# A three-layer graph network by one level of Strassen: halves of 1354 columns and a reordered schedule

## The reference

```python
h = maximum(layernorm(x), 0)
h = relu(adj @ (h @ W1) + b1)
h = relu(adj @ (h @ W2) + b2)
out = x + adj @ (h @ W3) + b3
```

## Time and profile before

| | us |
|---|---|
| median of 3 runs (lowest, highest) | 1641.04 (1639.48, 1642.48) |
| the profiled execution | 1642.07 |
| its span, first to last instruction | 1639.0 |
| TensorE busy | 1595.6 (97%) |
| VectorE busy | 868.2 (53%) |
| ScalarE busy | 605.7 (37%) |
| GpSimd busy | 472.0 (29%) |
| mean granted TensorE clock | 0.992 |
| HBM traffic | 191 GB/s over the span |

### The profile page before, as it was taken

How to read it: one execution, slowest core, us unless ns; L and a number is a source line. 1 busy time by engine, 2 the same in 40 slices (tenths; PEclk the granted TensorE clock), 3 DMA queues, 4 the chain that set the end, 5 groups by cost and what they waited for, 6 DMA issues and landing times.

```text
span 1639.0 us, 20964 instructions
## 1 busy us (share of the span) xinstructions
PE 1595.6 (97%) x7668; PEld 1371.4 (84%) x7668; DVE 868.2 (53%) x1359; ACT 605.7 (37%) x1072; POOL 472.0 (29%) x464
## 2 busy tenths in 40 slices
PE   6998999999999999999999999999999999999998
PEld 5886888988878888889898989878898887888898
DVE  7874332336652444444564446675554538766665
ACT  3442222233433333333333233444444435444443
POOL 6552554516665100000000006555302303121212
PEclk9998999999999999999999999999999999999999
DMA  7765665645566555444465568988654327787775
GB/s 263 238 220 167 216 226 170 202 122 168 171 203 206 179 160 157 136 133 137 125 189 161 159 204 276 330 301 290 204 155 113 103 81 211 203 270 225 213 223 173
DMA packets 199706, 314.85 MB, mean 192 GB/s; under 512 B 20768, under 2 KB 92792, under 8 KB 199604
## 3 DMA queue, kind: packets, MB, share of 16 engines
q1 hardware_dynamic: 163548, 230.48, 46.9%
q0 software_dynamic: 13760, 46.74, 8.4%
q10 hardware_dynamic: 22296, 36.30, 6.3%
HBM read 223.48 MB, written 89.72 MB: 191 GB/s over the span
## 4 chain that ended last, share of the span: by engine, by line
PE 88%; DMA 4%; DVE 3%; POOL 2%; issue 2%; ACT 1%; ACTq 0%; SPq 0%; POOLq 0%; DVEq 0%
PE ps L1551 29%; PE ps L1552 29%; PE ps L1553 29%; DMA prep<-P 1%; DMA T<-prep 1%; DVE ring L1245 1%; PE ps L1631 1%; DMA raw<-adjT 1%; DMA raw<-W2S 0%; POOL T L1450 0%; POOL prep L1496 0%; PE ps L1576 0%; DMA raw<-T 0%; POOL prep L1489 0%; POOL prep L1493 0%
## 5 line engine op out<-in xcount | busy, mean ns | idle before, releaser
L1245 DVE TENSOR_TENSOR ring<-raw,ring 128x512 fp32r<-128x512 f32 (+2 forms) x594 | 421.2, 722 | 459.6 <-ACT ring L1040 457.0
L1040 ACT CAST ring<-raw 128x512 fp32r<-128x512 f32 (+2 forms) x594 | 336.4, 575 | 597.0 <-PE ps L1553 489.1
L1551 PE MATMUL ps<-slots,still 128*128 128x512 f32 (+1 forms) x504 | 187.5, 372 | 23.9 <-DVE still L1208 15.3
L1552 PE MATMUL ps<-slots,still 128*128 128x512 f32 (+1 forms) x504 | 186.0, 369 | 0.0
L1553 PE MATMUL ps<-slots,still 128*128 128x512 f32 (+1 forms) x504 | 185.7, 369 | 0.0
L1551 PE MATMUL ps<-ring,even 128*128 128x512 f32 (+1 forms) x480 | 175.1, 365 | 1.1 <-DVE ring L1245 1.1
L1553 PE MATMUL ps<-ring,even 128*128 128x512 f32 (+1 forms) x480 | 175.0, 364 | 0.0
L1552 PE MATMUL ps<-ring,even 128*128 128x512 f32 (+1 forms) x480 | 174.9, 364 | 0.0
L1224 DVE TENSOR_TENSOR slots<-raw,slots 128x1024 fp32r<-128x1024 f32 (+1 forms) x63 | 83.3, 1323 | 152.2 <-ACT slots L999 152.2
L1551 PE MATMUL ps<-ring,S 128*128 128x512 f32 (+1 forms) x420 | 154.7, 368 | 6.5 <-DVE ring L1245 6.4
L1446 POOL DMA_DIRECT2D prep<-P x48 | 25.8, 540 | 463.9 <-DMA P<-U 432.8
(11 more groups left out here) (153 smaller groups left out, 2869.8 us busy)
## 6 DMA issues: line engine op xcount, KB each, us to landing
raw<-TS SPq DMA_DIRECT2D x160, 256.0 KB, 2.9
raw<-adjT SPq DMA_DIRECT2D x136, 256.0 KB, 3.2
raw<-adjT SPq DMA_DIRECT2D x42, 512.0 KB, 4.4
TS<-made SPq DMA_DIRECT2D x20, 1024.0 KB, 6.5
raw<-TS SPq DMA_DIRECT2D x80, 168.0 KB, 2.5
raw<-HS SPq DMA_DIRECT2D x50, 256.0 KB, 2.7
raw<-P SPq DMA_DIRECT2D x45, 256.0 KB, 3.9
raw<-adjT SPq DMA_DIRECT2D x68, 168.0 KB, 2.9
```

The lines of the kernel that those rows point to most:

```text
L1040: act.copy(hi, src).then_inc(hi_done, 1)
L1245: dve.tensor_tensor(lo, src, hi.bitcast(F32), ALU.subtract).then_inc(lo_done, 1)
L1551: pe.matmul(out, st_hi, mv_hi, start=start, stop=False)
L1552: pe.matmul(out, st_hi, mv_lo, start=False, stop=False)
```

## The change

Seven things change together.

- Halves of 1354 columns, chunks of 512, 512 and 330, no padding; rows in DRAM are 2708 floats (10832 bytes) where they were 2720 (10880 bytes).
- Start: the first adjacency tile comes as two halves (`a` = 0, 1) with a transfer, a cut and a set of matmuls each; one x tile is loaded ahead of it where there were three; ScalarE's root and centre of the first x tile come first.
- Pass 1: the tail tile (and in chunk 0 the short x tile) is cut after n = 10; the drains of a chunk come behind n = 0 of the next; the two first h1 ring tiles are cut ahead of the last chunk's drains.
- The short block's step in h1 and w3 is emitted 5 cuts later (before: 2 and 3).
- Two tail slots in turn.
- W2 phase: four spill buffers in chunk 0; the W3 loads in parts 1 to 4; GpSimd begins the T2 tiles of chunk c > 0 only when part 2 of chunk c - 1 is drained.
- Pass 3: x is added before the last group's drain for three of the four outputs, and their stores wait for the drain alone.

```diff
-WIDTH = (512, 512, 336)
+WIDTH = (512, 512, 330)
...
+            if first:
+                j.a = 0
+                k = tile("adj")
+                k.chunk, k.block, k.n, k.a, k.raw, k.slot = c, b, n, 1, j.raw, j.slot
...
+            if n == 10:
+                t = tile("tail")
+                t.chunk, t.block = c, SHORT
+                tails.append(t)
+                steps.append(("cut", t))
+                if c == 0:
+                    t.ready = take_x(SHORT).ready
...
-            if c > 0 and n == 1:
+            if c > 0 and n == 0:
                 steps.append(("drain", c - 1))
...
-            p.later(lag, emit(g, j))
+            p.later(lag if b != SHORT else LAG, emit(g, j))
...
-        g.tail = (p.tails, c, half, at["tail_freed"])
+        g.tail = (p.tails, c, half, at["tail_freed"][p.tails % 2])
...
-                if c == 1:
-                    extra = [lambda k=k: load_w3(k) for k in (2 * part, 2 * part + 1) if k < 8]
+                if c == 1 and 0 < part < 5:
+                    extra = [lambda k=k: load_w3(k) for k in (2 * part - 2, 2 * part - 1)]
...
+        spare = [("g", m if g.chunk == 0 else m % 2) for m in ms]
+        if part == 2:
+            at["paced", g.chunk] = p.drained
...
-            due = max(p.cuts + lag, w2_end + 11 + j)
+            due = max(p.cuts + (lag if b != SHORT else LAG), w2_end + 11 + j)
...
+        for where, half, side, last in {1: [(4, 0, 0, 1)], None: [(6, 1, 1, 4), (2, 0, 1, 5)],
+                                        4: [(0, 1, 0, 6)]}.get(part, []):
+            p.final += 2
+            p.final_of[g.chunk, last] = p.final
+            p.steps.append(("finish", (g.chunk, where, half, side, g.free_drained)))
...
+    spill_23 = place("spill_23", [P, 2, BANK], F32, left_at + 12 * H)
...
+    slot_tails = [place("slot_tail_0", [P, BANK], F32R, tail_at + 2 * BANK * 4),
+                  place("slot_tail_1", [P, BANK], F32R, tail_at + BANK * 4)]
...
+        first_cuts = [a for kind, a in steps[:2] if kind == "cut"]
...
-            for q in xs1[0:3]:
-                load_x(q)
+            load_x(xs1[0])
...
+                if j.a is not None:
+                    src = adjT[j.block * P:(j.block + 1) * P, columns(j.a, j.chunk)]
+                    sp.dma_start(raw1[:, j.raw % RAW1, j.a, 0:WIDTH[j.chunk]], src) ...
+                    if j.a == 1:
+                        load_x(xs1[1])
...
+            root(0)
+            centre(0)
             for kind, j in steps1:
                 if kind == "cut":
                     cut1(j)
                     continue
                 c = j
+                if c == CHUNKS - 1:
+                    for j in first_cuts:
+                        cut(j)
...
-                    act.wait_ge(finished, plan.final_of[g.chunk, g.part])
+                    if g.part == 1:
+                        act.wait_ge(finished, plan.final_of[g.chunk, 1])
+                    else:
+                        act.wait_ge(drained, number)
...
+                        if g.phase == "pass3" and part in (4, 5, 6):
+                            dve.wait_ge(finished, plan.final_of[g.chunk, part])
...
+                if c > 0:
+                    pool.wait_ge(drained, at["paced", c - 1])
                 for q in range(KF):
                     prep_moving(c, q)
...
+                    if j.a == 0:
+                        order = [(m, a) for a in range(2) for m in range(KF)]
```

More of the change, by code:

```diff
@@ L196, in take_raw, with take_x @@
         raw_user[j.raw % RAW1] = j
+        raw_counts[j.raw % RAW1] += 16
+        j.raw_count = raw_counts[j.raw % RAW1]
     xs = []
+    def take_x(block):
+        q = tile("x")
+        q.block, q.q = block, len(xs)
+        xs.append(q)
+        steps.append(("cut", q))
+        return q
     for c in range(CHUNKS):
         mine = []
-        for n, b in enumerate(BLOCKS):
-            j = tile("adj" if b != SHORT else "tail")
+        for n, b in enumerate(BLOCKS[:-1]):
+            j = tile("adj")
             j.chunk, j.block, j.n = c, b, n
[L204 to L212, removed]
+            first = c == 0 and n == 0
+            take_raw(j)
+            j.slot = slots
+            slots += 1
+            user = slot_user[j.slot % RING1]
+            j.place_freed = user.freed if user else None
+            slot_user[j.slot % RING1] = j
+            used += b != 20
+            j.freed = ("group", 8 * (c + 1)) if b == 20 else ("slot", used)
             mine.append(j)
@@ L215, in plan_pass1 @@
             if c == 0:
[L216 to L221, removed]
+                j.partner = take_x(b)
+                j.ready = j.partner.ready
+            if first:
+                j.a = 0
+                k = tile("adj")
+                k.chunk, k.block, k.n, k.a, k.raw, k.slot = c, b, n, 1, j.raw, j.slot
+                k.raw_count = j.raw_count
+                k.partner = j
+                j.partner = k
+                raw_user[j.raw % RAW1] = k
+                steps.append(("cut", k))
+            if n == 10:
[5 more added lines that the diff above has]
+                    t.ready = take_x(SHORT).ready
             if c == 1 and n % 2 == 1 and 2 < n < 18:
@@ L231, in plan_pass1 @@
     assert sum(j.kind == "weight" for j in tiles) == 8
-    return tiles, steps, by_chunk, xs
+    return tiles, steps, by_chunk, tails, xs
 def plan_main():
@@ L562, in store @@
                     p.store(("e", finals[1] + m))
-                p.steps.append(("store", (g, finals)))
-            p.later(4, store)
+                p.steps.append(("store", (g, finals, number)))
+            p.later(4 if part == 1 else 2, store)
     h1_phase(2)
@@ L751, in x_column @@
         def x_column(n, which):
-            rows = slice(0, REP if n == SHORT else P)
+            rows = slice(0, REP if xs1[n].block == SHORT else P)
             k = ("-mean", "v", "root", "r", "vrr", "step", "scale").index(which)
@@ L835, in _ @@
                     else:
-                        sp.wait_ge(lo1_done, chunks1[j.chunk - 1][SHORT].ready)
+                        sp.wait_ge(lo1_done, tails1[j.chunk - 1].cut + 1)
                     src = adjT[j.block * P:N, :].rearrange("p (a n) -> p a n", a=2)
@@ L978, in cut1 @@
                     tile, rows = x_tile(j)
-                    hi = still_tail1[rows, :] if n == SHORT else still[:, j.block, 0, :]
+                    hi = still_tail1[rows, :] if j.block == SHORT else still[:, j.block, 0, :]
                     act.activation(hi, tile, ACT.Relu, scale=x_column(n, "scale")).then_inc(hi1_done, 1)
-                    if n + 2 <= SHORT:
+                    if n == 0:
+                        root(1)
+                    elif n + 2 <= SHORT:
                         root(n + 2)
@@ L1331, in _ @@
                     ms, busy = a[1:3] if w2 else ((0, 1), a[1])
+                    spare = a[3] if w2 else None
                     y = KF if w2 else 2
@@ L1341, in _ @@
                         elif w2:
-                            C = spill(m % 2, c)
+                            C = spill(spare[i][1], c)
                         else:
@@ L1526, in _ @@
                     continue
-                g, finals, number = a
-                c = g.chunk
-                half = 0 if g.part in (1, 5) else 1
-                side = 0 if g.part in (1, 6) else 1
+                c, where, half, side, number = a
                 for m in range(2):
```

212 lines of the change are left out of this document (119 added, 93 removed).

## The result

| | us |
|---|---|
| changed kernel, median of 4 runs (lowest, highest) | 1619.78 (1613.98, 1623.72) |
| kernel before, median of 4 runs (lowest, highest) | 1640.26 (1637.91, 1642.48) |
| ratio, 95% interval | 0.9873 (0.9834 to 0.9911) |
| the profiled execution, changed (before) | 1616.77 (1642.07) |
| its span | 1615.0 (1639.0) |

The change is faster, by 20.5 us of medians and 25.3 us of profiled executions. The forecast was 35.7. The direction holds, and so does the range, by 0.2 us: its end is 1620. The size doesn't. Of the six outcomes with a price, B (1617) and E (1615) lie nearest to the median.

What follows compares the result with a forecast made beforehand. The prediction took TensorE's stream of matmuls and its breaks to bound the kernel. Gains of 44.0 us less losses of 8.3 gave 35.7 off the profiled 1642.07, and 1.0 more off for the median: 1605.4, range 1594 to 1620.

Steps and rivals of the forecast that it cites:

- B: W2 phase: GpSimd's steps stay at 17.7 us, costing 14.7 and 3.4 of clock instead of 6.3; 1617, chance 0.14.
- E: Pass 1: second block and block behind n = 10 stand 5 us with half clock, 13.4 not 4.0; 1615, chance 0.10.
- chunk 1 of the W2 phase: GpSimd's new wait makes part 2's last T2 tile late: 4.6 and 1.7 of clock, 6.3 us lost (0 to 18).
- A: W2 phase: the paced preparation is in time (steps at or under 14 us), 6.3 us given back; 1599, chance 0.27.
- P: W2 phase: time of one GpSimd preparation step; 14.0 us breaks even, 15.1 was taken, 17.7 was chunk 1's before.
- By the same reckoning chunk 2 is about in balance; I put nothing.: W2 phase, chunk 2: GpSimd's new wait was put at no loss.
- Start and n = 10: Pass 1, chunk 0: start gains 5.0 us after a stall near 2; n = 10 gains 6.2, with 2.0 charged.
- Start of pass 3: End of w3: emitting the short block two cuts later removes TensorE's ring wait and half clock, 4.3 us gained.
- Width: Third chunk, 2204 matmuls: six columns less save 2.5 ns each, 5.4 us gained (bounds 0 and 5.6).
- Rival C: Third chunk: the narrower width gives nothing because of a fixed cost per matmul; 1611, chance 0.04.
- Rows of 10832 bytes: DRAM transfers: unaligned rows taken to cost nothing; estimate under 2% per transfer, some 1 us in the W2 phase.
- Rival D: W2 phase and pass 3: unaligned rows lengthen every transfer, 63 us more at 1.4 times; 1668, slower, chance 0.05.

Runs made afterwards that it cites:

- e1: The changed kernel itself timed again, beside e2 to e4 on the same chip: 1618.52 us, ratio to before 0.9864.
- e2: The changed kernel without GpSimd's wait for the drain of part 2 of the chunk before: 1608.81 us, ratio to before 0.9804.
- e5: The changed kernel with GpSimd waiting for the drain of part 1 instead of part 2 of the chunk before: 1609.72 us, ratio to before 0.9810.
- e3: The changed kernel with the third chunk of 336 columns and padded rows of 2720, as before: 1618.61 us, ratio to before 0.9866.
- e7: The changed kernel with TensorE alone reading other widths (256 to 334 columns) of the third chunk, output incomplete or stale: one execution 1613.21 us.
- e6: The changed kernel with chunk 0's short x tile at n = 14 and w3's short-block copies issued by GpSimd: 1612.07 us, ratio to before 0.9826.
- e4: The kernel before with only the third chunk narrowed to 330 columns (rows of 10832 bytes): 1638.15 us, ratio to before 0.9978.
- e9: e8 with a third chunk of 336 columns and padded rows: 1605.26 us, ratio to before 0.9788.
- e11: The same kernel as e8, timed again beside e9 on the same chip: 1603.10 us, ratio to before 0.9772.
- e8: The changed kernel with the edits of e5 and e6 together: 1601.99 us, ratio to before 0.9764.

## Why the prediction was right or wrong, point by point

**Right.** What bounds the kernel: TensorE's stream and its breaks, 98% busy after. The boundaries of pass 1 but for those 1.9 us, the two early h1 tiles, the short block in h1 and the narrower third chunks were put at 15.7 and brought 16.8 (14.8 in e1). Some 1.7 of that is luck: 512 matmuls of pass 1 ran at 150.0 ns where seven of nine profiles have 153.3. The half clock near 129, 143 and 347 of before is gone. The spill stall went (4.2 forecast, 4.7 measured), though e2 shows that this needs the wait as well: with four buffers alone a wait of 0.8 stays at the spill and the rest moves to the ring. The end brought 3.0 where 1.8 was forecast.

**Right by two errors: chunk 1 of the W2 phase.** Forecast 6.3 lost, measured 6.5, at the place named: before the fourth tile of part 2. But a step of GpSimd took 16.9 us ((1092.24 - 1041.54) / 3, the first additions of the steps), not the 15.1 that I chose. Between GpSimd's first load and the ready tile I had 4 x 15.1 + 9.8 = 70.2 us; measured 1106.0 - 1035.7 = 70.3. The fourth step needn't be whole: its last tile is made 5.9 us after its first addition, at 1098.1. The reserve in one term paid for the other; that was luck. Of the rivals, A (in time) is false, and B's P (17.7) was nearer to the measured 16.9 than mine, but the loss was 6.5 us where B had 18.1.

**The step that failed most: "By the same reckoning chunk 2 is about in balance; I put nothing."** Chunk 2 lost 4.7 us. The reckoning wasn't carried out; the term stood at nothing without a sum. GpSimd begins its tiles after part 2 of chunk 1, at 1117.02, and that part is now itself late by the wait in chunk 1; the fourth step begins its additions at 1162.40, and ring casts wait 4.34 us for T2 tiles at 1174.22 while TensorE needs 7.2 us for a part:

```profile
1171.24 3.65 SPq L982 DMA_DIRECT2D raw<-T  x5
...
1174.72 0.50 DVE L1297 TENSOR_TENSOR ring<-raw,ring 128x330 fp32r<-128x330 f32 x1 [5.23 <-ACT ring L1071]
...
1179.09 0.50 DVE L1297 TENSOR_TENSOR ring<-raw,ring 128x330 fp32r<-128x330 f32 x1 [1.07 <-ACT ring L1071]
1179.50 0.91 DVE L1442 TENSOR_TENSOR parts<-ps,parts 128x330 f32<-128x330 f32 x2
```

SyncE, whose loads stand in order behind a T2 tile, issues none for the ring between 1160 and 1171.24. The chain passes from loads to casts, to DVE's cuts, and to a drain (1179.50) that stands behind a cut in DVE's order; TensorE waits for that drain until 1180.56. e2 and e5, where GpSimd begins earlier, show the late start to be the cause: both losses are gone at once, 5.5 to 5.9 us in chunk 2 and 6.5 in chunk 1.

**Start and n = 10: two stalls under-sized.** The second block stood for 3.5 us with half clock behind it (1.7), where I had 2.0; the first matmul came at 8.47, as worked out. For n = 10 I charged 2.0 with bounds 0 and 5, counting DVE's added work (3.8) against its slack (1.4). It cost 3.6, and half clock behind it in four of the five other profiles that have this stall (e1, e2, e3, e5; not e7). The two stalls with the half clock seen here make 3.5 + 1.7 + 3.6 = 8.8 us in place of the 4.0 charged, nearly all of the 5.0 missing in the first stretch. The work was right, and the forecast missed that it stands between statistics that ScalarE waits for, so DVE couldn't use what slack it had. That was rival E's mechanism, with two thirds of its price (13.4); e6 takes the second stall away and gets 4.0 to 5.2 us in that chunk.

**Start of pass 3: 4.3 forecast, some 0.9 there, and 8.4 against 4.7 in all.** Chunk 0 gained 1.9, of which the second tail slot has about 1.0, as in the two chunks behind it (1.2, and 1.6 with the width). I counted on the emission two cuts later to cover the copies. In the trace they are issued at 1336.41, and TensorE stands 2.45 us at 1340.47 with the same 1.54 us of issue in the chain. The break stands 30 matmuls into pass 3 where before it stood 18 in, two ring tiles later, as far as the step was moved: moving the step moved the stall. The 1.7 of half clock was no gain to be had by itself either: e3 and e5 have none there, but a further wait of 0.8, and the chunk takes 106.99 and 106.97 us, the same as here. Moving the issue to GpSimd (e6) leaves two breaks of 1.0 and 0.8 us and no half clock behind them.

**Width: the term was mis-sized, 5.4 forecast, 2.7 by e4 (4.0 in its own stretches).** I drew a line between two paces and gave the fixed cost as the lower bound, not as a thing that can hold in one phase and not in another. Pass 2 gives 2.6, where the line has 2.3. Pass 1 gives nothing in most executions, pass 3 0.3 of 1.1. Rival C is half true. In the changed kernel the 2.7 didn't show in the time (e1 1618.52, e3 1618.61).

**Rows of 10832 bytes.** Rival D is false as a whole: e4 has these rows and is faster than before. The T2 loads land in 4.2 us (5.1 before), the stores in 3.6 (4.3), GpSimd's loads in 5.4 (5.3). The views of DMA issues after:

```profile
prep<-P POOLq DMA_DIRECT2D x32, 256.0 KB, 5.4
T<-prep POOLq DMA_DIRECT2D x32, 256.0 KB, 3.6
raw<-T SPq DMA_DIRECT2D x32, 256.0 KB, 4.2
```

Single packets of 2048 bytes have a median of 84 ns in every profile, and a mean of 103.5 ns before, 103.2 in e4, 104.1 after and 102.9 in e3. The prediction's estimate by the Trainium skill, "DMA: Bandwidth & Descriptors", section "How a descriptor splits into AXI transactions", was under 2%; with -0.3% in one pair and 1.2% in the other the means are too near to nothing to bear that rule out or to refute it.

One stretch leaves the question open. In chunk 1 of the W2 phase, whose T2 tiles have 512 columns in every kernel, GpSimd's steps are shorter with the aligned rows in all three comparisons: 17.7 us before and 18.2 in e4; 16.3 in e3 and 16.9 in e1; 16.1 in e9, 17.3 in e11 and 18.2 in e8. In chunk 0 there is no such trend (15.4 to 16.4 us with either). These are single profiles, and no run moves the rows without the width.

**The sum.** Against 10.4 us missing in the profiled pair, chunk 2 of the W2 phase with its width holds 5.5, the start with n = 10 5.0, pass 3 with the width there 3.7 and chunk 1 0.2; the middle gives back 1.1, chunk 0 of the W2 phase 0.5, the end and what lies outside the span 2.5.

## What to carry over

A wait added to pace an engine is dated by the last tile it must deliver, for each later round in turn, since a late round starts the next one late; here one part earlier was worth 8.8 us. Before work is moved into a busy engine's order, look at who waits for the step that comes behind it, not only at that engine's slack. And a saving per instruction read from two far widths is a mean: measure it at the width itself, by phase, before it is multiplied by the count.

## What the runs showed of the hardware

- With a weight load for each, float32r, at full granted clock, the mean distance of matmuls is columns / 2.4 ns + 13.3 at four widths: 120.0 at 256, 146.7 at 320, 153.3 at 336, 226.7 at 512. It is no straight line between: 148.9 at 326, 150.0 at 332. 330 columns run at 150.0 or at 153.3, by stretch and by execution.
- The length of a break didn't decide by itself whether half clock came with it. Breaks of 3.5, 3.6, 3.3 and 2.6 us had it, for 3.42 or 6.83 us. The block behind n = 10 had it behind a break of 3.2 in e5 and not behind one of 3.6 in the changed kernel's profile. The break of 2.6 at the start of pass 3 had it in the changed kernel, e1, e2 and e7, and not in e3 and e5. In e8 a break of 2.5 at 16.4 had none. So a break is priced with nothing, 1.7 or 3.4 us more behind it.
